# Sixteen gathers of segment ends moved into each edge convolution, and the start of a convolution moved into the stage before it

## The chip, the cores and the metric

The kernel runs on one core of a Trainium2 chip. The metric is the device time of one execution in microseconds (us), given as the median of several runs. The profile is of one execution. Its engines are PE (TensorE; PEld is its weight load), DVE (VectorE), ACT (ScalarE), POOL (GpSimd) and SP (SyncE, which here only issues DMAs). SPq, ACTq and POOLq are the DMA-issuing instructions of an engine.

## What is computed

A graph network on 3125 nodes with 96 features and 53125 directed edges, sorted by their target. Four layers follow each other, each with a residual and a layer norm. The second is the one that the change is about: two edge convolutions with a segment maximum.

```python
def _egnn_conv(x, src, dst, edge_attr, W_msg, W_edge, W_root, b):
    msg = x[src] @ W_msg + edge_attr @ W_edge
    agg = jax.ops.segment_max(msg, dst, num_segments=x.shape[0])
    agg = jnp.where(jnp.isneginf(agg), 0.0, agg)
    return agg + x @ W_root + b
...
x = _layernorm(x + _L0_gnn_ref(x, edge_index), axis=-1)      # two hops of the normalised adjacency
c1 = leaky_relu(_egnn_conv(X, src, dst, edge_attr, W1_msg, W1_edge, W1_root, b1))
c2 = leaky_relu(_egnn_conv(c1, src, dst, edge_attr, W2_msg, W2_edge, W2_root, b2))
x = _layernorm(x + c2)                                       # the second layer
x = _layernorm(x + _L2_gnn_ref(x, edge_index), axis=-1)      # sixteen hops
x = _layernorm(x + _L3_gnn_ref(x, edge_index, ...), axis=-1) # graph convolution, graph norm, another
```

## The kernel before

Nodes lie in 25 tiles of 125 (`P` by `T`); a node array is [125, 25, 96]. The program is a row of stages. Each stage is a block in which all five engines run their own instruction lists, joined by semaphores; between two blocks stands a barrier of all engines, so a block starts when the last engine has finished the one before. In order of time:

1. `build_counts` makes the dense count matrix, degrees and the row in which each node's segment ends.
2. `hops` "l0": two hops, PE-bound. Beside them `AttrHalves` splits the edge attributes into two 16-bit halves: SP loads `l0a_raw` (L642), POOL casts and subtracts (L665, L671), SP stores the halves (L649, L653), 50 rounds through 3 buffers. Behind these on SP stand the ten stores of the state, `state_parked` (L808).
3. `node_product` "c1w" (L934 on): PE turns node tiles (L1011) and multiplies them with W_msg and W_root (L1044); ACT copies the turned tiles (L1053) and writes the high halves of the messages (L1086); DVE writes their low halves (L1129) and the root term (L1131). SP stores `messages` in five cuts (L998), ACT stores `root_parked` (L1078). At the end SP and ACT wait until these stores have landed.
4. `edge_conv` "c1": 26 iterations of 16 tiles of 128 edges. In each, POOL fetches the messages' rows of 11 tiles by indirect DMA (L1240) into `gathered`, which holds two iterations; the other 5 tiles are taken by PE with one-hot matrices (L1273), which DVE makes (L1339) from the source numbers that SP loads (L1190) and ACT offsets (L1392). PE adds attributes and rows in `c_msg` (L1252 to L1262), DVE takes the running maximum along the edges (L1349), PE turns it back (L1300), ACT copies it (L1407) and stores it to `running_max` in DRAM (L1409), 104 groups of 512 edges. `room` (L1225) lets POOL run at most two iterations ahead of PE. At the end ACT waits for its last stores.
5. `node_product` "c2w": now each group of five node tiles must first be put together. POOL gathers the row at which each node's segment ends from `running_max`, one indirect DMA a tile, 25 in all (L1449); SP loads the root term (L1455); DVE adds them and applies leaky ReLU (L1461, L1462). Then turns and products as in c1w. The groups are put into DVE's list between the products by `groups_before` (L971), so that a turn of four tiles waits for the group that holds the last of them.
6. `edge_conv` "c2", as 4.
7. `sixteen_and_one` "l2": first the same 25 gathers with root and state loads, then per group DVE's sum, norm and scaling; PE starts when two groups have gone through. Then sixteen hops and the first product of the last layer, PE-bound throughout.
8. `node_product` "g2w" and `hops` "g2".

The heads of an edge convolution in code (SP, then ACT); DVE's part is three small operations on the edge weights (L1357 to L1361) and then the first one-hots:

```python
for k in range(4):
    sp.dma_start(wf[32 * k:32 * k + 32, :], c["w"][w_edge]).then_inc(s_w, 16)
load_srcs(0, TE)
load_srcs(1, TE)
...
act.wait_ge(s_init, 1)
offset_srcs(0)
act.wait_ge(s_we, 2)
act.wait_ge(s_hot, NC)
offset_srcs(1)
...
evacuate(0)
```

## Time and profile before

| | |
|---|---|
| median of 3 runs | 2112.2 us (2110.45 to 2113.62) |
| the profiled execution's own time | 2111.14 us |
| its span on the core | 2109.1 us |
| busy share of the span | PE 91%, PEld 89%, DVE 61%, ACT 32%, POOL 35% |
| instructions | 55767, of these POOL 756, PE 22813 |
| mean granted clock of TensorE | 0.958 of full speed |

Stages in the trace, us from the span's start: hops "l0" to 234.6; c1w 236.1 to 254.3; the first edge convolution from 259.1, its products from 266.2; c2w from 650.1 to 694.6; the second edge convolution from 698.7, its products from 705.6; the last layers from 1088.5. The stage after the second convolution has its first product at 1117.8 and PE has little idle time from there to 2101.

How to read it: a busy share is an average over stages. PE is the bound in the hops, which are half of the span; what the change touches lies around and inside the two edge convolutions, where PE, POOL and the gaps between the blocks matter one by one. In the rows below, a row of the timeline is: start, length, engine, line, operation, out<-in, shapes, count, and in brackets how long the engine had been idle before it and what ended that. Several neighbours of one kind are merged into one row (x10), whose length then runs from the first start to the last end.

### The profile page before, as it was taken

What the parts mean: (1) busy time and instruction counts of PE and PEld (TensorE: products, weight loads), DVE (VectorE), ACT (ScalarE), POOL (GpSimd) and SP (SyncE); (2) the same over time, 40 slices, a digit from 0 to 9 for tenths busy, and PEclk for the clock granted to TensorE, in tenths of its full rate; (3) what the DMA queues carried; (4) which work ended last, traced back from release to release, by engine and by line L of the source; (5) the groups of instructions that cost most, each with busy time, mean ns of one, the idle gap of its engine ahead of it and who ended that gap; (6) DMA issues with size and microseconds to landing.
All of it is one profiled execution on the core that took longest, in us unless ns stands there. A gap on an engine that the chain in (4) does not pass through costs nothing. (4 is left out here: it accounts for less than half of the span.)

```text
span 2109.1 us, 55767 instructions
## 1 busy us (share of the span) xinstructions
PE 1910.3 (91%) x22813; PEld 1868.7 (89%) x22813; DVE 1277.6 (61%) x3480; ACT 670.2 (32%) x1913; POOL 734.3 (35%) x756
## 2 busy tenths in 40 slices
PE   4579699999994799999956999999999999999968
PEld 3579689999994699999956999999999999999958
DVE  8955578888883588888857444444444444446435
ACT  6843322222221122222212333333333333334234
POOL 2467277777764577777742000000000000000000
PEclk9899899999996899999987999999999999999979
DMA  3034456666664466666650000000000000000001
GB/s 82 1 89 136 114 136 173 168 169 175 166 167 107 118 169 168 177 168 166 177 138 22 2 2 2 2 2 2 2 2 2 2 2 2 2 2 2 2 3 24
DMA packets 150815, 160.32 MB, mean 76 GB/s; under 512 B 43421, under 2 KB 139288, under 8 KB 150561
## 3 DMA queue, kind: packets, MB, share of 16 engines
q1 hardware_dynamic: 98169, 80.74, 14.6%
q0 software_dynamic: 20464, 32.18, 8.1%
q10 hardware_dynamic: 31928, 43.84, 5.8%
q8 instruction: 180, 2.95, 0.6%
q14 instruction: 74, 0.61, 0.1%
HBM read 100.90 MB, written 55.75 MB: 74 GB/s over the span
## 5 line engine op out<-in xcount | busy, mean ns | idle before, releaser
L1240 POOL DMA_INDIRECT c_gathered<-messages,idx_all x572 | 560.2, 979 | 174.9 <-issue 138.3
L1273 PE MATMUL c_taken<-rows,c_hot 125*128 125x192 f16 x6500 | 572.7, 247 | 25.2 <-DVE c_hot L1339 25.2
L1273 PEld LDWEIGHTS c_taken<-rows,c_hot 125*128 125x128 f16 x6500 | 537.0, 98 | 26.1 <-issue 25.8
L1503 PE MATMUL l_ps<-rows,counts 125*128 125x192 f16 x5625 | 471.4, 248 | 40.1 <-DVE rows L1579 39.6
L1503 PEld LDWEIGHTS l_ps<-rows,counts 125*128 125x128 f16 x5625 | 468.2, 99 | 42.1 <-DVE rows L1579 40.8
L1339 DVE TENSOR_SCALAR c_hot<-c_offset_srcs 125x640 f16<-125x640 f16 x1300 | 381.2, 349 | 97.3 <-PE c_taken L1273 84.8
L1503 PE MATMUL l_ps<-l_u,counts 125*128 125x192 f16 x5000 | 413.8, 246 | 0.0
L1503 PEld LDWEIGHTS l_ps<-l_u,counts 125*128 125x128 f16 x5000 | 412.6, 98 | 0.0
L1606 DVE SCALAR_TENSOR_TENSOR l_uf<-l_ps,l_cf,l_wide 125x96 f32<-125x96 f32 x400 | 127.1, 318 | 325.7 <-ACT l_wide L1546 325.6
L1349 DVE TENSOR_TENSOR_SCAN c_scanned<-c_mask,c_scanned,c_msg 96x512 f32<-96x512 bf16 x208 | 264.9, 1273 | 34.9 <-PE c_msg L1262 26.2
L1546 ACT ACTIVATE l_wide<-l_ps,l_cl 125x96 f32<-125x96 f32 x400 | 135.9, 340 | 299.7 <-PE l_ps L1503 299.0
L1407 ACT ACTIVATE c_back<-c_tr 128x384 f32<-128x384 f32 x208 | 102.0, 490 | 402.1 <-PE c_tr L1300 386.9
L1612 DVE TENSOR_TENSOR l_uf<-l_uf,l_wide 125x96 f32<-125x96 f32 x400 | 103.0, 258 | 13.6
L1300 PE MATMUL c_tr<-ident,c_scanned 96*128 96x96 f32 x832 | 103.3, 246 | 4.7 <-DVE c_scanned L1349 4.7
L1550 ACT ACTIVATE l_u<-l_uf 125x96 f16<-125x96 f32 x200 | 56.6, 283 | 135.4 <-DVE l_uf L1612 135.4
L1399 ACT ACTIVATE c_evacuated<-c_taken 128x384 f16<-128x384 f32 x156 | 62.5, 435 | 114.1 <-PE c_taken L1273 102.2
L1615 DVE SCALAR_TENSOR_TENSOR l_u<-l_u,l_uf 125x96 f16<-125x96 f16 x200 | 51.8, 259 | 69.8 <-ACT l_u L1550 69.8
L1550 ACT ACTIVATE rows<-l_uf 125x96 f16<-125x96 f32 x175 | 49.5, 283 | 118.4 <-DVE l_uf L1612 118.4
L1300 PEld LDWEIGHTS c_tr<-ident,c_scanned 96*128 96x128 f32 x832 | 81.1, 141 | 5.7 <-ACT c_back L1407 5.7
L453 PE MATMUL count_ps<-b_hot,b_low 125*128 125x125 f16 x625 | 53.1, 238 | 34.3 <-DVE b_hot L562 33.9
L1252 PE MATMUL c_msg<-c_attr,c_we 128*96 128x512 f16 x208 | 79.5, 382 | 4.9 <-DMA c_attr<-attr_halves 4.8
L405 ACT CAST counts<-count_ps 125x500 f16<-125x500 f32 (+1 forms) x157 | 77.9, 638 | 15.5 <-PE count_ps L441 15.4
(268 smaller groups left out, 1789.5 us busy)
## 6 DMA issues: line engine op xcount, KB each, us to landing
running_max<-c_back ACTq DMA_DIRECT2D x208, 192.0 KB
c_attr<-attr_halves SPq DMA_DIRECT2D x412, 64.0 KB
c_mask<-segment_mask SPq DMA_DIRECT2D x206, 96.0 KB
c_gathered<-messages,idx_all POOLq DMA_INDIRECT x572
c_srcs<-sources SPq DMA_DIRECT2D x50, 160.0 KB
l0a_raw<-in_ea_t SPq DMA_DIRECT2D x50, 132.8 KB
attr_halves<-l0a_hi SPq DMA_DIRECT2D x50, 66.4 KB, 2.0
attr_halves<-l0a_lo SPq DMA_DIRECT2D x50, 66.4 KB, 2.1
```

The costliest lines, as they stand in the source:

```text
L1240: pool.indirect_dma_start(out=gat[:, i % 2, j, :], out_offset=None, in_=c["y_d"], in_offset=bass.IndirectOffsetOnAxis(ap=idx_all[:, i * IT ...
L1252: pe.matmul(msg[0:F, k, :], we[:, :], attr[:, n % AHEAD, :], start=True, stop=False)
L1273: return pe.matmul(acc[:, (NB * i + j // 2) % ACCS, j % 2 * (2 * F):(j % 2 + 1) * (2 * F)], hot[:, slot + k, j * ET:(j + 1) * ET], y[:, t, :],
L1300: last = pe.transpose(tr[0:ET, g % 2, j * F:(j + 1) * F], scanned[0:F, g % 2, j * ET:(j + 1) * ET], ident[0:F, 0:F])
L1339: last = v.tensor_scalar(hot[:, SLOTS[h % len(SLOTS)] + k, :], off[:, :], float(t * P - SRC_MID), None, ALU.is_equal)
L1349: v.tensor_tensor_scan(scanned[0:F, k, :], mk[:, n % AHEAD, :], msg[0:F, k, :], scanned[0:F, 1 - k, GW - 1:GW], ALU.add, ALU.max).then_inc ...
L1407: act.activation(back[:, g % 2, :], tr[0:ET, g % 2, 0:GT * F], ACT.Copy, scale=1.0 / YS).then_inc(s_back, 1)
L1503: return pe.matmul(ps[:, t % HB, 0:2 * F], at[:, k, t * P:t * P + 128], u[hop % 2][:, k, :], start=(k == 0), stop=(k == T - 1), skip_group ...
L1546: act.activation(clo[:, b, :], ps[0:P, b, F:2 * F], ACT.Copy, scale=(cl if hop < count else cl_next)[:, t:t + 1]).then_inc(s_clo, 1)
L1550: act.activation(u[(hop + 1) % 2][:, t, 0:F], uf[:, t, :], ACT.Copy, scale=1.0 / LO).then_inc(s_hi, 1)
L1606: v.scalar_tensor_tensor(uf[:, t, :], ps[0:P, b, 0:F], (cf if hop < count else cf_next)[:, t:t + 1], clo[:, b, :], ALU.mult, ALU.add).then ...
L1612: v.tensor_tensor(uf[:, t, :], uf[:, t, :], xa[:, t, :], ALU.add).then_inc(s_uf, 1)
```

## The change

- The array of rows, `conv_rows` [128, 25, 192] of 16-bit values, is now kept for the whole program. It holds the state in the first layer, in a convolution the gathered rows (22 of its 25 tiles) and part of the evacuated ones, and after it the segment ends as [128, 25, 96] of 32 bits. So result tile t lies where gathered tile t lay.
- When POOL has issued all 286 gathers of messages, it goes on inside the same block with 16 of the 25 gathers of segment ends (`EARLY`), in five pieces of 4, 4, 3, 4 and 1. Ahead of each piece it loads a number from `need` and waits for the message group that last read these rows and for as many stores to `running_max`, on both parities, as the number says. The number is made by three DVE operations in the first convolution, one value per node tile, and loaded by SP in iteration 2. The 9 other gathers stay where they were.
- `ConvHead`: the load and scaling of the edge weights, the first load of sources and its offset are now done in `node_product`. On SP the five loads stand ahead of the stores of messages; on ACT the offset stands first in its list; on DVE the three weight operations stand ahead of everything; POOL does the iota.
- `node_product` no longer waits for its stores. In the convolution POOL waits for the 10 stores of messages ahead of its first gather, DVE for the 10 stores of the root term after three of its eight chunks of one-hots, ACT ahead of its first evacuation.
- In the hops "l0" SP also writes 16 blocks of zeros (196608 bytes each) over the last 16 groups of `running_max`, one ahead of each of the first 16 rounds of the halves; POOL clears the source.

The core of the diff:

```diff
+EARLY = 16
+CUTS = (0, 6, 12, 18, 22, T)
+N_STORED = 32 * (len(CUTS) - 1)
+CLEARED = 16
...
         with ExitStack() as s1:
-            xs = s1.enter_context(nc.sbuf_tensor("x_state", [P, T, F], F32))
-            build_counts(ctx, src, dst, xs, x)
-
+            head = ConvHead(ctx, s1)
+            head.begin("c1h", "W1_edge")
+            node_product(ctx, "c1w", xs, "W1_msg", "W1_root", "b1", y16=y, parked=stored, head=head)
+            result = ConvResult(ctx, "c1r", rows)
+            edge_conv(ctx, "c1", y, result, head, ends=True)
+            head.begin("c2h", "W2_edge")
             with ExitStack() as st:
-                hs = hop_state(ctx, st, "l0", teleports=False)
-                stored = hops(ctx, "l0", hs, xs, 1.0, 0.0, 2, norm=xs, out=xs_d, halves=AttrHalves(ctx, st, "l0a"), later=True)
-            node_product(ctx, "c1w", xs, "W1_msg", "W1_root", "b1", y16=y, parked=stored)
-        edge_conv(ctx, "c1", "W1_edge", y, ends=True)
-        with ExitStack() as st:
-            c1 = st.enter_context(nc.sbuf_tensor("c1", [128, T, F], F32))
-            conv = ConvResult(ctx, st, "c1r", c1)
-            node_product(ctx, "c2w", c1[0:P, :, :], "W2_msg", "W2_root", "b2", y16=y, conv=conv)
-        edge_conv(ctx, "c2", "W2_edge", y)
+                node_product(ctx, "c2w", result.res[0:P, :, :], "W2_msg", "W2_root", "b2", y16=y, conv=result, head=head)
+            result = ConvResult(ctx, "c2r", rows)
+            edge_conv(ctx, "c2", y, result, head)
...
             load(n)
         for n in range(NPREP):
             at_n = slice(n * PREP, (n + 1) * PREP)
+            if n < CLEARED:
+                sp.wait_ge(self.s_zeros, 1)
+                sp.dma_start(self.scan_v[EP // GW - 1 - n, :, :], self.zeros[:, :]).then_inc(self.s_cleared, 16)
             sp.wait_ge(self.s_hi, n + 1)
             sp.dma_start(self.to_d[0][:, at_n], self.hi[:, n % DEEP, :]).then_inc(self.s_put_hi[n % DEEP], 16)
...
                     for a, b in zip(cuts, cuts[1:]):
                         sp.wait_ge(s_o, -(-b // per))
                         for ps in (slice(0, WHOLE), slice(WHOLE, P)):
-                            sp.dma_start(yv[ps, a:b, :], y[ps, a:b, :]).then_inc(s_st, 16)
-                    sp.wait_ge(s_st, 32 * (len(cuts) - 1))
+                            sp.dma_start(yv[ps, a:b, :], y[ps, a:b, :]).then_inc(head.s_y, 16)
                     if parked:
                         sp.wait_ge(*parked)
 
...
                         act.wait_ge(s_o, -(-z // per))
                         for ps in (slice(0, WHOLE), slice(WHOLE, P)):
-                            act.dma_start(c["root_d"][ps, a:z, :], root[ps, a:z, :]).then_inc(s_parked, 16)
+                            act.dma_start(c["root_d"][ps, a:z, :], root[ps, a:z, :]).then_inc(head.s_root, 16)
 
                     done, left = 0, list(zip(cuts, cuts[1:]))
                     for b, r in enumerate(batches):
+                    head.vector(v, wf)
                 if graph_norm:
                     for i, r in enumerate(turns):
...
+        self.w_edge = w_edge
+        self.s_w, self.s_wf, self.s_we, self.s_init, self.s_srcs, self.s_off, self.s_y, self.s_root = (
+            self.c["sem"](f"{tag}_{n}") for n in ("w", "wf", "we", "init", "srcs", "off", "y", "root"))
+
+    def load_srcs(self, sp, i, width):
+        sp.wait_ge(self.s_off, i + 1)
+        at_edge = (i * IT + FROM_POOL) * ET
+        sp.dma_start(self.srcs[:, 0:width], self.c["src_d"][:, at_edge:at_edge + width]
+                     .to_broadcast([128, width])).then_inc(self.s_srcs, 16)
+
+    def offset_srcs(self, act, i):
+
+        act.wait_ge(self.s_srcs, 16 * i + 16)
+        act.activation(self.off[:, :], self.srcs[0:P, :], ACT.Identity, bias=self.lane[:, 0:1]).then_inc(self.s_off, 1)
+
+    def sync(self, sp, wf):
+        for k in range(4):
+            sp.dma_start(wf[32 * k:32 * k + 32, :], self.c["w"][self.w_edge]).then_inc(self.s_w, 16)
+        self.load_srcs(sp, 0, self.TE)
+
+    def gpsimd(self, pool):
+        pool.sem_inc(self.s_off, 1)
+        pool.iota(self.lane[:, :], pattern=[[0, 1]], base=0, channel_multiplier=-1,
+                  allow_small_or_imprecise_dtypes=True).then_inc(self.s_init, 1)
+
+    def scalar(self, act):
+        act.wait_ge(self.s_init, 1)
+        self.offset_srcs(act, 0)
+
+    def vector(self, v, wf):
+        we = self.we
+        v.wait_ge(self.s_w, 64)
+        v.tensor_scalar(wf[:, :], wf[:, :], YS, None, ALU.mult).then_inc(self.s_wf, 1)
+        v.wait_ge(self.s_wf, 1)
+        v.tensor_copy(we[:, :], wf[:, :]).then_inc(self.s_we, 1)
+        v.wait_ge(self.s_we, 1)
+        v.tensor_tensor(we[64:AE, :], wf[64:AE, :], we[64:AE, :], ALU.subtract).then_inc(self.s_we, 1)
+
+
...
+        def taken_rows(j, n):
+
+            k = (j // 2 * 2) % 4
+            return tak[:, j - 2:j - 2 + n, :] if k else rows[:, 2 * FROM_POOL + j - j // 4 * 2:2 * FROM_POOL + j - j // 4 * 2 + n, :]
+
...
                 for s in (s_msg, s_scan, s_tr, s_back):
                     pool.sem_inc(s, GT)
...
+                pool.wait_ge(s_need, 16)
+                if ends:
+                    pool.wait_ge(s_none, 17)
+                pool.sem_inc(s_gate, 1)
+                for k in range(2):
+                    for g, tiles in enumerate(by_dma):
+                        early = [k * FROM_POOL + j for j in tiles if k * FROM_POOL + j < EARLY]
+                        if early:
+                            stored = pool.value_load(need[0:1, early[-1]:early[-1] + 1], min_val=32, max_val=16 * (N_IT * GT // 2 + 1))
+                            pool.wait_ge(s_msg, (N_IT - 2 + k) * GT + g + 1 + GT)
+                            pool.sem_inc(s_gate, 1)
+                            for parity in range(2):
+                                pool.wait_ge(s_st[parity], stored)
+                                pool.sem_inc(s_gate, 1)
+                            for t in early:
+                                result.gather(pool, t)
 
...
+                one_hots(0, 0, 1, 2)
+                v.wait_ge(head.s_root, N_STORED)
+                one_hots(0, *range(3, NC))
                 v.memset(scanned[0:F, 1, GW - 1:GW], 0.0).then_inc(s_zero, 1)
                 v.wait_ge(s_zero, 1)
-                v.wait_ge(s_w, 64)
-                v.tensor_scalar(wf[:, :], wf[:, :], YS, None, ALU.mult).then_inc(s_wf, 1)
-                v.wait_ge(s_wf, 1)
...
-                offset_srcs(0)
-                act.wait_ge(s_we, 2)
                 act.wait_ge(s_hot, NC)
-                offset_srcs(1)
+                head.offset_srcs(act, 1)
+                act.wait_ge(head.s_root, N_STORED)
                 if ends:
...
 
 
-    def __init__(self, c, st, tag, res, root=None):
-        self.c, self.res = c, res
-        self.root = st.enter_context(c["nc"].sbuf_tensor(f"{tag}_root", [P, T, F], F32)) if root is None else root
+    def __init__(self, c, tag, rows):
+        self.c, self.rows, self.res, self.root = c, rows, rows[:, :, :].bitcast(F32), None
         self.s_maxima = [c["sem"](f"{tag}_maxima{g}") for g in range(T // G)]
         self.s_root = [c["sem"](f"{tag}_root{g}") for g in range(T // G)]
         self.s_ready = c["sem"](f"{tag}_ready")
 
+    def gather(self, pool, t):
+        pool.indirect_dma_start(out=self.res[:, t, :], out_offset=None, in_=self.c["scan_d"],
+                                in_offset=bass.IndirectOffsetOnAxis(ap=self.c["end_idx"][:, t:t + 1], axis=0),
+                                ).then_inc(self.s_maxima[t // G], 16)
+
     def gpsimd(self, pool):
-        for t in range(T):
-            pool.indirect_dma_start(out=self.res[:, t, :], out_offset=None, in_=self.c["scan_d"],
-                                    in_offset=bass.IndirectOffsetOnAxis(ap=self.c["end_idx"][:, t:t + 1], axis=0),
-                                    ).then_inc(self.s_maxima[t // G], 16)
+        for t in range(EARLY, T):
+            self.gather(pool, t)
 
```

Two places show how the lists move. POOL, first edge convolution to the next stage (`c_gathered` before and `conv_rows<-messages` after are the gathers of messages; `<-running_max` those of segment ends). Before:

```order
L1215 UNCONDITIONAL_BRANCH
L1222 IOTA c_lane 125x1
L1240 DMA c_gathered<-messages,idx_all 128x192 x286
L1184 UNCONDITIONAL_BRANCH
L100 ISA
L1093 UNCONDITIONAL_BRANCH
L1449 DMA c<-running_max,end_idx 128x96 x25
```

and in the changed kernel:

```order
L1316 DMA conv_rows<-messages,idx_all 128x192 x286
L1329 TENSOR_LOAD c_need
L1329 ISA x2
L1533 DMA conv_rows<-running_max,end_idx 128x96 x4
L1329 TENSOR_LOAD c_need
L1329 ISA x2
L1533 DMA conv_rows<-running_max,end_idx 128x96 x4
L1329 TENSOR_LOAD c_need
L1329 ISA x2
L1533 DMA conv_rows<-running_max,end_idx 128x96 x3
```

Of the 25 gathers behind the block's end (a branch), 16 stand ahead of it now, each piece behind a load of a number. ACT at the start of c1w, before:

```order
L1048 UNCONDITIONAL_BRANCH
L1053 ACTIVATE c1w_xt<-c1w_pt 96x500 x2
L1086 ACTIVATE rows<-c1w_py 125x2x96 x2
L1053 ACTIVATE c1w_xt<-c1w_pt 96x500
L1086 ACTIVATE rows<-c1w_py 125x2x96 x2
```

and in the changed kernel:

```order
L1069 UNCONDITIONAL_BRANCH
L1190 ACTIVATE head_offset_srcs<-head_srcs,head_lane 125x640
L1074 ACTIVATE c1w_xt<-c1w_pt 96x500 x2
L1109 ACTIVATE rows<-c1w_py 125x2x96 x2
L1074 ACTIVATE c1w_xt<-c1w_pt 96x500
```

The offset, which waits for the load of sources, stands ahead of the copies without which PE has nothing to multiply. c2w is built in the same way.

## Rows read from the trace of the kernel before

**Rows 1.** Timeline of hops l0 and c1w; columns as told above, in time and profile
```profile
225.57 9.82 SPq L808 DMA_DIRECT2D state_parked<-x_state  x10
...
233.32 1.29 DVE L757 TENSOR_SCALAR x_state<-x_state,l_n_less,l_n_y 125x96 f32<-125x96 f32 x5
...
236.89 0.32 SPq L992 DMA_DIRECT2D c1w_b_row<-in_w_b  x1
...
240.20 2.92 PE L1044 MATMUL c1w_py<-c1w_w,c1w_xt 96*125 96x192 f32 x8 [2.24 <-DMA c1w_b_row<-in_w_b]
```

**Rows 2.** Timeline, end of c1w and head of the first edge convolution
```profile
254.30 1.73 ACTq L1078 DMA_DIRECT2D root_parked<-c1w_root  x3
...
260.42 1.06 POOL L1240 DMA_INDIRECT c_gathered<-messages,idx_all  x1 [0.58 <-issue]
...
260.91 4.64 SPq L1190 DMA_DIRECT2D c_srcs<-sources  x2
...
264.35 0.83 ACT L1392 ACTIVATE c_offset_srcs<-c_srcs,c_lane 125x640 f16<-125x640 f16 x1 [10.94 <-DMA c_srcs<-sources]
...
266.15 11.80 PE L1273 MATMUL c_taken<-rows,c_hot 125*128 125x192 f16 x125 [13.09 <-DVE c_hot L1339]
```

**Rows 3.** Waits of SP's own queue: engine line, released by, us in total, times, longest
```profile
SPq L978 <- DMA messages<-rows: 5.5, 2, 2.8
```

**Rows 4.** Timeline of POOL in the first edge convolution; its last message gather is 627.40
```profile
386.83 0.95 POOL L1240 DMA_INDIRECT c_gathered<-messages,idx_all  x1 [0.30 <-PE c_taken L1273]
...
587.12 1.01 POOL L1240 DMA_INDIRECT c_gathered<-messages,idx_all  x1 [0.30 <-PE c_taken L1273]
...
627.40 0.94 POOL L1240 DMA_INDIRECT c_gathered<-messages,idx_all  x1 [0.30 <-issue]
```

**Rows 5.** Timeline, end of the first edge convolution and c2w
```profile
647.12 0.33 ACTq L1409 DMA_DIRECT2D running_max<-c_back  x1
...
650.06 4.07 SPq L1455 DMA_DIRECT2D c1r_root<-root_parked  x10
...
659.09 0.66 DVE L1461 TENSOR_TENSOR c1r_root<-c1r_root,c 125x480 f32<-125x480 f32 x1 [13.26 <-DMA c<-running_max,end_idx]
...
666.97 2.77 PE L1044 MATMUL c2w_py<-c2w_w,c2w_xt 96*125 96x192 f32 x8
...
673.27 2.77 PE L1044 MATMUL c2w_py<-c2w_w,c2w_xt 96*125 96x192 f32 x8
...
694.36 0.25 DVE L1131 TENSOR_TENSOR c1r_root<-c2w_py,c2w_b_row 125x96 f32<-125x96 f32 x1
```

**Rows 6.** Timeline of SP and DVE where SP reads two loop counts and starts a loop
```profile
77.61 0.13 DVE L552 TENSOR_SCALAR b_further<-b_rounds 1x1 int32<-1x1 f32 x1
...
80.70 0.33 SPq L303 DMA_DIRECT2D b_win<-edge_values  x1
```

**Rows 7.** Windows: stretch us, busy us and count by engine, PE clock, DMA share, GB/s
```profile
121.00:165.00 44.00, 41.39 (x471) 41.01 (x472) 25.82 (x48) 13.52 (x41) 32.88 (x41) 0.91 0.47 129
...
668.00:684.00 16.00, 10.61 (x38) 9.46 (x37) 6.37 (x16) 3.73 (x9) 10.52 (x12) 0.50 0.31 73
```

**Rows 8.** DMA queue, kind: packets, MB, share of 16 engines; q10 carries ACT's stores
```profile
q10 hardware_dynamic: 31928, 43.84, 5.8%
```

**Rows 9.** Timeline of the second edge convolution: first and last message gather, first product
```profile
699.97 0.95 POOL L1240 DMA_INDIRECT c_gathered<-messages,idx_all  x1 [0.53 <-issue]
...
705.55 6.64 PE L1273 MATMUL c_taken<-rows,c_hot 125*128 125x192 f16 x57 [12.13 <-DVE c_hot L1339]
...
1065.08 0.94 POOL L1240 DMA_INDIRECT c_gathered<-messages,idx_all  x1 [0.30 <-issue]
```

**Rows 10.** Timeline, start of sixteen_and_one
```profile
1088.49 0.75 SPq L1455 DMA_DIRECT2D l_wide<-root_parked  x2
...
1096.74 0.66 DVE L1461 TENSOR_TENSOR l_wide<-l_wide,l_u 125x480 f32<-125x480 f32 x1 [7.50 <-DMA l_u<-running_max,end_idx]
...
1103.07 0.66 DVE L1461 TENSOR_TENSOR l_wide<-l_wide,l_u 125x480 f32<-125x480 f32 x1 [2.58 <-DMA l_u<-running_max,end_idx]
```

120 lines of the change are left out of this document (68 added, 52 removed).

## The prediction

> **What bounds the kernel now.** The busy shares say PE everywhere, but they are averages; the change touches neither the hops nor the 26 iterations of a convolution as such, so I went to the timeline at the seams, then to POOL's row of gathers, then to SP's waits. Three things are to be seen. First, a seam costs about 12 us without products: the last root store of c1w is issued at 256.03 (254.30 + 1.73), the first product of the convolution starts at 266.15 [rows 2]. The block waits for stores to land (SP up to 2.8 [rows 3]), then for weights, sources (3.44 from issue at 260.91 to the offset at 264.35), offset 0.83 and one-hots. Second, behind a convolution DVE waits 13.26 for the first five segment ends in c2w [rows 5], and 7.50 and 2.58 in the next stage [rows 10]. Third, POOL is not idle enough to be ignored: a gather is 0.94 and the 0.30 behind it, so an iteration of 11 takes it at least 13.7; the first nine took 14.05 each (260.42 to 386.83), the next fourteen exactly 14.31 (to 587.12) [rows 2, 4]. That steady 14.31 I read as PE's pace, to which the limit of two iterations holds POOL. Its last gather starts at 627.40, 23 before the block ends.
>
> **The sum, step by step**, against the profiled execution's 2111.14.
>
> *Zeros in the hops.* SP's halves are through at 225.57, when the ten state stores begin; the last two need the norm that ends at 234.61 [rows 1]. Eight stores at some 0.4 (ten loads take 4.07 [rows 5]) must be out by then, which leaves 5.8 of slack. A block of zeros is a store of the form of ACT's: those took 5.8% of 16 engines times 2109.1 over 31928 packets [rows 8], 61 ns a packet, so 128 packets over 16 engines are 0.5 and the sixteen 7.8. Nothing hidden: +2.0; all of it in free time of the DMA engines, which are busy 0.47 there [rows 7]: 0. I take the middle, **+1.0**. POOL's clearing is one instruction in 11 us in which POOL has 0.25 of the time free [rows 7].
>
> *c1w.* ACT's list now begins with an offset that needs sources loaded behind seven small DMAs. SP is through with the third at 237.21 [rows 1]; four more at 0.41 give 238.9, then 3.4 and 0.83 as in rows 2: 243.1. Only then comes the first copy of turned tiles, some 0.6 (an estimate: 500 columns where the offset has 640), so products start at 243.8 for 240.20 [rows 1]. **+3.7**, between 3.0 (copy overlapped) and 4.5. POOL's iota and DVE's weights lie inside that wait.
>
> *First convolution.* Between two blocks the barrier costs 0.7: state stores end at 235.39, SP's third load of the next block is at 236.89, less two issues [rows 1]. So the block starts at 256.7 and PE, one-hots being 1.0 ahead of it (265.18 to 266.15 [rows 2]), at 257.9: 8.2 earlier. But POOL must see the stores landed, 256.03 + 2.8 [rows 2, 3], and gathers from 259.3, only 1.1 earlier. The gathers are needed at PE's new time; eleven of them, 3.4 to land by the sources' row, are there at 275.2, and the third message group, some 19 behind PE's start, asks at 277: I see no stall, with 2 to spare. From here POOL decides: 9.5 behind the pace at which PE held it, it gets its own, between 13.7 and the 14.05 seen while unheld. I take 14.0, near the measured end: last gather at 259.3 + 25 x 14.0 + 12.5 = 621.8, 5.6 earlier. Behind it come 16 gathers at 1.25 (20.0), the 0.94 of the last, 0.7 barrier and five loads of a number. No row shows such a load on POOL; SP needed 2.96 for two of them, three loops and a third load [rows 6], so one is between 0 and 1.0, and with no nearer row I take 0.5, 2.5 in all. Block end 621.8 + 24.1 = 645.9 for 650.06: **-4.2**. PE's side would end at 647.12 - 8.2 plus the 2.9 that follow now [rows 5], 641.9, so POOL's tail is the new end of the block. Its waits for messages and stores cost nothing: tile 15 ends about 64% through the edges, stored long before. DVE's and ACT's waits for the root stores end at 258.8, when DVE has just made its three chunks. The Trainium skill (DMA: Bandwidth & Descriptors, "Latency and other measured facts") gives a floor of about 600 ns for such a load; by that the five are 3.0 and each block ends 0.5 later.
>
> *c2w.* Here 16 of 25 segment ends are there at the start, but others aren't. SP issues ten root loads (4.07), three weights, four edge weights (2.9) and the sources, at 7.0; offset done at 11.2. DVE now waits for the edge weights ahead of its first group, to about 9.6, adds two groups (4 x 0.66), 12.3, and PE turns: products 13.4 into the block for 16.9 (650.06 to 666.97 [rows 5]). After that the pace is 6.30 per group (666.97 to 673.27), and I credit nothing against it: five gathers are 6.25, but turn 1.1, two products' batches 2.8, ACT 0.3, DVE 0.6 and the next group 1.4 are 6.2 in a ring as well (small ones estimated from c1w's and these rows), because `groups_before` puts the group behind the batch. Rows 7 show why it is slow: PE 66% busy at a granted 0.50, the 1.2 GHz level. **-3.8**. The Trainium skill (TensorE: Matmul & The Clock Gate, "What's actually happening") says that the throttled state is the default and activity releases it; without gather waits it would speak for the 2.4 GHz level here. The row with PE at 66% shows no release, and the ring keeps that share.
>
> *Second convolution.* The same: PE 7.8 earlier, POOL 1.1 (699.97 to 698.9), last gather 698.9 + 350 + 12.5 = 1061.4 for 1065.08 [rows 9], block end 1085.5 for 1088.49 [rows 10]: **-3.0**.
>
> *Start of the sixteen hops.* DVE's first group waits for root rows only, some 3.1 after their issue at 1088.49, for 1096.74; the 2.58 ahead of the second go too [rows 10]. Afterwards DVE is never kept by a gather. **-7.7**, between 6.5 and 8.5. The nine gathers left are out 11 us into the block, ahead of the fourth group.
>
> Nine gathers left in c2w cost nothing for the same reason; the doubled use of `conv_rows` adds no instruction.
>
> Sum: +1.0 + 3.7 - 4.2 - 3.8 - 3.0 - 7.7 = **-14.0**, 2097. The profiled execution lies 1.1 under the median of the runs, 2112.2; I leave that in the range. A measurement of this kernel can tell 0.2%, 4.2 us, from no change: faster is below 2108.0, slower above 2116.4.
>
> **The rivals.**
> *POOL doesn't catch up (slower).* If 14.31 is POOL's own pace beside a busy DVE and not PE's hold, the earlier PE gives nothing back and the tail stands behind it in full. With loads at 1.0 the blocks end at 259.3 + 357.8 + 12.5 + 26.6 = 656.2 and at 1095.8: +6.1 and +7.3, sum +6.6, **2118**. Each 0.1 of pace is 5.0 us over both convolutions, so the sign turns at 14.28. For it: fourteen iterations at 14.31. Against: their evenness, their releaser PE, and 14.05 earlier. Chance 0.10; another 0.10 for paces of 14.15 to 14.28, **2107**.
> *The clock rises in c2w.* A ring with turn 0.6 and products 1.5 at 2.4 GHz is 4.4; some four rings save 7: sum -21, **2090**. Against: rows 7. Chance 0.15. With POOL at 13.7 and free loads, both blocks ending with PE, it would be 2081, the far end.
> *The zeros are in the way.* If every load of attributes had to wait for a whole block of zeros, at the 3.4 of the sources' load [rows 2], sixteen cost 54 less 5.8: sum +33, **2144**. The order on SP speaks against it: each round's load is issued ahead of the next zeros. The Trainium skill (DMA: Bandwidth & Descriptors, "Issuing engines are not separate DMA queues") has all issuers share 16 DMA engines, so zeros are never free where those are full; here they are half free. Chance 0.03.
>
> **How the numbers follow.** My forecast, paces up to 14.15, has 0.62. Faster: 0.62 + 0.15 and half of the 2107 case, 0.82. Slower: the part of the first rival beyond 2116.4 and the zeros, 0.07. The same: 0.11. The range runs from the clock case with a faster POOL, 2084, to the 2107 case and its upper side, 2110; it leaves out the slower cases and the far end.
>
> **What would show it.** POOL's last gather of messages near 621.8 + 4.7 (the two stages ahead are later), then pieces of segment ends with gaps of 0.5 to 1 and the next block within 1 us of the last; The first product of each convolution 2 us after the last store issued in the stage before, where it was 10. c1w's first product at about 244.8, with ACT idle on a DMA. c2w still at 0.50 for most of its length and some 27 us from first product to last root term. The first group of the sixteen hops some 3 after the block's start, with no gather wait on DVE. I am wrong if POOL's iterations stay at 14.31 from the start, if the halves' end moves past 231, or if c2w's clock is 1.0.

## The result: 0.24% slower, where 0.7% faster was forecast

| | before | changed |
|---|---|---|
| median of 20 runs each | 2110.89 us (2106.37 to 2116.13) | 2115.42 us (2111.32 to 2120.7) |
| ratio | | 1.0024, 95% interval 1.0018 to 1.0031 |
| the profiled execution's own time | 2111.14 us | 2115.44 us |
| its span | 2109.1 us | 2113.6 us |
| mean granted clock of TensorE | 0.958 | 0.956 |
| POOL instructions | 756 | 757 |

The forecast was 2097, with a range of 2084 to 2110. The result lies above it. The change made the kernel slower: the interval leaves out 1, though its lower end is just inside the 0.2% that I had called the same.

Where the time went, stage by stage, in the two profiled executions. A stage ends where the last instruction of its slowest engine ends or the next block starts, and the spans are differences of such times in the two timelines ([rows 2, 5, 9, 10] and the rows below):

| stretch | before, us | changed, us | difference | forecast |
|---|---|---|---|---|
| start to the end of c1w's root terms on DVE | 254.3 | 257.95 | +3.7 | +4.7 |
| from there to the start of c2w's block | 395.8 | 402.7 | +6.9 | -4.2 |
| c2w, to its last root term | 44.6 | 41.1 | -3.4 | -3.8 |
| from there to the start of sixteen_and_one | 393.9 | 399.3 | +5.4 | -3.0 |
| its head, to PE's first product | 29.3 | 21.6 | -7.7 | -7.7 |
| the rest | 991.3 | 991.0 | -0.3 | 0 |

So four of six rows are right to 1 us, and both convolutions are wrong by 8 to 11 us. First the heads. The timeline of the changed kernel at the start of c1w and across the seam into the first convolution (start, length, engine, line, operation, what it waited for):

```profile
235.55 1.87 PE L1032 MATMUL c1w_pt<-ident,conv_rows 125*96 125x125 f32 x8 [7.11 <-PEq L809]
241.77 0.83 ACT L1190 ACTIVATE head_offset_srcs<-head_srcs,head_lane 125x640 f16<-125x640 f16 x1 [10.08 <-DMA head_srcs<-sources]
243.22 2.89 PE L1065 MATMUL c1w_py<-c1w_w,c1w_xt 96*125 96x192 f32 x8 [5.80 <-ACT c1w_xt L1074]
...
258.01 1.56 ACTq L1101 DMA_DIRECT2D root_parked<-c1w_root  x3
260.15 0.34 SPq L1184 DMA_DIRECT2D head_srcs<-sources  x1
...
261.16 5.12 PE L1366 MATMUL c_taken<-rows,c_hot 125*128 125x192 f16 x31 [4.41 <-DVE c_hot L1432]
262.48 1.16 POOL L1316 DMA_INDIRECT conv_rows<-messages,idx_all  x1 [26.75 <-DMA messages<-rows]
```

The product at 243.22 waits for ACT, which waits for the sources: 3.0 later than in [rows 1], the lower end of what was forecast (3.7, from 3.0 to 4.5). In return the first one-hot product starts 1.6 behind the last root store (259.57), where it was 10.1 in [rows 2]. POOL's first gather is 2.1 later than before, since it waits for the stores of a stage that ended 3.7 later.

Now the end of the convolution. POOL's timeline:

```profile
629.75 0.94 POOL L1316 DMA_INDIRECT conv_rows<-messages,idx_all  x1 [0.30 <-PE c_taken L1366]
631.00 0.94 POOL L1533 DMA_INDIRECT conv_rows<-running_max,end_idx  x1 [0.30 <-issue]
...
649.72 0.94 POOL L1533 DMA_INDIRECT conv_rows<-running_max,end_idx  x1 [0.30 <-issue]
660.64 1.60 SPq L1543 DMA_DIRECT2D c2w_root<-root_parked  x4
660.74 0.13 POOL L1199 IOTA head_lane<- 125x1 f32 x1 [10.07 <-POOLq L105]
```

The early gathers follow the messages' without a gap and at 1.25 each, so the five loads and their waits cost nothing. But between POOL's last gather (650.66) and the next block (660.64) nothing at all runs for 10 us, on any engine. I had put 0.7 there. A row of the timeline does not say what an engine does while it closes a block; the view of one source line does, and the line is that of the block itself. It lists the queue's own instructions: engine, operation, count, duration in ns (least, median, most), start of the first and of the last. The changed kernel at the end of the first convolution:

```profile
L1267 POOLq DRAIN  x1: 21565/21565/21565, 638.2 to 638.2; - x1
...
L1267 PEldq DRAIN  x1: 550/550/550, 640.7 to 640.7; - x1
...
L1267 ACTq DRAIN  x1: 8/8/8, 644.2 to 644.2; - x1
```

And the same view of the kernel before, at the same place:

```profile
L1184 POOLq DRAIN  x1: 13617/13617/13617, 622.6 to 622.6; - x1
...
L1184 ACTq DRAIN  x1: 8/8/8, 649.2 to 649.2; - x1
```

```profile
DMA packets 0, 0.00 MB, mean 0 GB/s; under 512 B 0, under 2 KB 0, under 8 KB 0
```

The other seam is alike: there the DRAIN starts at 1079.9 and takes 20.3, to 1100.2, 9.1 behind a last gather that ends at 1091.10; the next block starts at 1101.07. Its head went as forecast:

```profile
1103.85 0.66 DVE L1549 TENSOR_TENSOR l_wide<-l_wide,conv_rows 125x480 f32<-125x480 f32 x1 [2.03 <-DMA l_wide<-root_parked]
...
1108.42 0.65 DVE L1549 TENSOR_TENSOR l_wide<-l_wide,conv_rows 125x480 f32<-125x480 f32 x1
```

In c2w the products start 14.2 into the block, and PE's granted clock is 0.50 there, the 1.2 GHz level; it rises to 0.61 on average in the last 16 us (timeline and windows). Over all of PE's work in c2w it is 0.57, in the changed kernel (672.4 to 700.75) as in the kernel before (661.0 to 693.4):

```profile
674.86 2.77 PE L1065 MATMUL c2w_py<-c2w_w,c2w_xt 96*125 96x192 f32 x8
...
680.88 2.77 PE L1065 MATMUL c2w_py<-c2w_w,c2w_xt 96*125 96x192 f32 x8
```

```profile
668.00:684.00 16.00, 8.33 (x28) 6.85 (x28) 6.40 (x15) 3.88 (x8) 3.53 (x4) 0.50 0.11 29
684.00:700.00 16.00, 11.38 (x45) 10.85 (x46) 7.18 (x20) 4.25 (x12) 0.00 (x0) 0.61 0.35 92
```

### The profile page after: what moved, and what is told of

Same layout as the page of the kernel before. It is cut to its first block and busy times, and to the rows that moved or that the text cites. A ratio compares the mean times of both kernels' runs of the same rounds, so it can differ in the third digit from the quotient of the medians.

```text
span 2113.6 us, 55849 instructions
## 1 busy us (share of the span) xinstructions
PE 1909.1 (90%) x22813; PEld 1867.1 (88%) x22813; DVE 1274.3 (60%) x3483; ACT 670.9 (32%) x1913; POOL 732.5 (35%) x757
## 5 line engine op out<-in xcount | busy, mean ns | idle before, releaser
L1316 POOL DMA_INDIRECT conv_rows<-messages,idx_all x572 | 560.1, 979 | 233.5 <-issue 146.9
L1432 DVE TENSOR_SCALAR c_hot<-head_offset_srcs 125x640 f16<-125x640 f16 x1300 | 374.8, 345 | 96.4 <-PE c_taken L1366 89.0
L1591 PE MATMUL l_ps<-conv_rows,counts 125*128 125x192 f16 x5000 | 413.8, 246 | 0.0
L1591 PEld LDWEIGHTS l_ps<-conv_rows,counts 125*128 125x128 f16 x5000 | 412.6, 98 | 0.0
L1355 PE MATMUL c_msg<-ident,conv_rows 128*96 128x128 f16 x728 | 108.9, 219 | 0.0
L1354 PE MATMUL c_msg<-ident,conv_rows 128*96 128x128 f16 x728 | 108.8, 218 | 0.0
L1355 PEld LDWEIGHTS c_msg<-ident,conv_rows 128*96 128x96 f16 x728 | 83.8, 122 | 19.5
L1638 ACT ACTIVATE conv_rows<-l_uf 125x96 f16<-125x96 f32 x200 | 56.5, 283 | 135.8 <-DVE l_uf L1700 135.8
L1703 DVE SCALAR_TENSOR_TENSOR conv_rows<-conv_rows,l_uf 125x96 f16<-125x96 f16 x200 | 51.8, 259 | 69.9 <-ACT conv_rows L1638 69.9
L1354 PEld LDWEIGHTS c_msg<-ident,conv_rows 128*96 128x96 f16 x728 | 86.1, 123 | 0.4 <-DMA conv_rows<-messages,idx_all 0.4
```

The costliest lines, as they stand in the source:

```text
L1316: pool.indirect_dma_start(out=gat[:, i % 2, j, :], out_offset=None, in_=c["y_d"], in_offset=bass.IndirectOffsetOnAxis(ap=idx_all[:, i * IT ...
L1354: pe.matmul(to, row[:, 0:F], ident16[:, :], start=False, stop=False)
L1355: last = pe.matmul(to, row[:, F:2 * F], ident16[:, :], start=False, stop=(j == GT - 1))
L1432: last = v.tensor_scalar(hot[:, SLOTS[h % len(SLOTS)] + k, :], off[:, :], float(t * P - SRC_MID), None, ALU.is_equal)
L1591: return pe.matmul(ps[:, t % HB, 0:2 * F], at[:, k, t * P:t * P + 128], u[hop % 2][:, k, :], start=(k == 0), stop=(k == T - 1), skip_group ...
L1638: act.activation(u[(hop + 1) % 2][:, t, 0:F], uf[:, t, :], ACT.Copy, scale=1.0 / LO).then_inc(s_hi, 1)
```

## The experiments

What had to be found out: whether the hole belongs to gathers in arrears, to a toll of the DRAIN itself, or to the loads and register waits; what the early gathers and the moved head are each worth; and whose pace POOL's 14.2 us for 11 gathers is. Each run stands beside runs of the kernel before on the same chip. The first four ran on a chip on which before takes 2348.16 (15 runs), with 18 us for an iteration of a convolution and PE often waiting for its instructions. Their totals are read against that number only; the DRAINs are read as they stand.

### No early gathers, and five

```diff
-EARLY = 16
+EARLY = 0
```

> EARLY is 0: no segment end is gathered inside a convolution, all else of the change stays (head, zeros, waits for stores). Theory A (gathers in arrears): the block waits for POOL's DRAIN, which lasts until its gathers are really through, some 8 to 9 us behind the last row of the timeline, at 1.33 a gather. Then 16 gathers fewer end the DRAIN of the first convolution at 638.5 for 659.8, ACT's last store (DRAIN of ACT at 644.2) sets the end, and c2w starts at 645.1 for 660.6 (-15.5); the second convolution's block ends 13.3 earlier against its start; the sixteen hops' second group has to wait for ten gathers again (+7.2). Total 2094 to 2096. Theory B (the pace only, as in the prediction, the hole being something else that comes with the head or the new array): the hole stays about 10 us behind POOL's or ACT's last work, c2w starts at 650 or later, total 2105 to 2112.

```diff
-EARLY = 16
+EARLY = 5
```

> EARLY is 5, else as the changed kernel. Theory A: eleven gathers fewer at 1.33 end POOL's DRAIN at 645.1, 0.9 later than ACT's end of 644.2, so c2w starts at 646.0; in the second convolution the DRAIN (1100.2 less 14.6) is 1.3 ahead of ACT's end, so 13.3 are saved against the start; the second group of the sixteen hops waits for five gathers more than now, +2. Total 2115.4 - 14.6 - 13.3 + 2.0 = 2089.5, between 2087 and 2093, faster than both kernels. Theory B (a fixed 10 us follow any gather of segment ends inside the block): POOL's last gather is at 636.9, the hole ends at 647, c2w starts at 647.5, and this is 2091 to 2094 too, so this run prices the version and the lone gather tells A from B.

Measured: 2341.24 with none (ratio to before 0.997, 0.9956 to 0.9984) and 2331.57 with five (0.9922, 0.9901 to 0.9943). Both beat the kernel before, on a chip where the absolute numbers of the expectation don't apply. With none, POOL's DRAIN ended 7.8 behind its last gather and ahead of ACT; with five it ended 8.2 behind, still ahead of ACT. In both the next block started 0.8 behind ACT's DRAIN (with none, 762.09 for 761.3), so the moved head and the new array bring no hole behind ACT. A hole of 10 us behind POOL's last gather would be hidden in both runs, so they don't tell arrears from a toll. What they show is that with none or five of the 16 the change is a gain.

### The loads and waits without the gathers

```diff
                             for parity in range(2):
                                 pool.wait_ge(s_st[parity], stored)
                                 pool.sem_inc(s_gate, 1)
-                            for t in early:
-                                result.gather(pool, t)
...
-        for t in range(EARLY, T):
+        for t in range(T):
             self.gather(pool, t)
```

> The five pieces keep their loads of a number and their waits, but gather nothing; all 25 gathers stand in the next stage. Theory A: loads and waits are the sequencer's and cost nothing, POOL's DRAIN ends at 638 to 639 and the blocks end with ACT, c2w at 645 to 646, total within 1 us of the run with EARLY 0 (2094 to 2096). Theory C (register loads, waits on a register and their extra instructions make the hole): the hole of 10 us stays behind POOL's last wait (644), c2w starts at 654 or later, total 2112 or more.

Measured: 2345.19 (one run, before 2348.16). The end of the first convolution, in POOL's timeline and in the block's line:

```profile
740.98 0.99 POOL L1316 DMA_INDIRECT conv_rows<-messages,idx_all  x1 [1.19 <-remote]
766.56 0.13 POOL L1199 IOTA head_lane<- 125x1 f32 x1 [24.59 <-POOLq L105]
```

```profile
L1267 POOLq DRAIN  x1: 7823/7823/7823, 757.3 to 757.3; - x1
...
L1267 ACTq DRAIN  x1: 8/8/8, 765.6 to 765.6; - x1
```

The block ends with ACT, so theory C falls: loads and waits make no hole. But they hold the DRAIN back until 757.3, and that tells against theory A. By then POOL had been without a gather for 15 us, and the queue of POOL's own DMAs (q0) moved no packet from 744 on. No transfer was in arrears, and the DRAIN took 7.82 all the same: what takes this time begins only when the DRAIN is asked for. The Trainium skill (Perfetto Trace Analysis, "DMA Instruction — SWDGE (GPSIMD)") says that POOL's row of such a DMA ends with its descriptors, not with the data; that would explain a short lag (in the changed kernel the last packet moved at 651.8, 1.2 behind the last row), but not 7.82 us when no data was moving.

### One gather behind PE's last turn

```diff
-EARLY = 16
+EARLY = 1
...
-                            pool.wait_ge(s_msg, (N_IT - 2 + k) * GT + g + 1 + GT)
+                            pool.wait_ge(s_tr, N_IT * GT + GT)
```

> EARLY is 1 and that gather waits until PE has turned its last group (641), so POOL is idle for 11 us ahead of it and then issues one gather. Theory A (arrears of a long row of gathers): the arrears are worked off while POOL is idle, the DRAIN ends 2 to 2.5 behind the lone gather, near 644.5, c2w starts at 645 to 646, total 2094 to 2096. Theory B (a fixed 8 to 10 us behind the last indirect DMA of a block that has had hundreds): the DRAIN ends at 650 to 652, c2w starts 6 to 7 later than in the run with EARLY 0, total 2107 to 2110.

```profile
759.98 0.94 POOL L1533 DMA_INDIRECT conv_rows<-running_max,end_idx  x1 [19.17 <-DMA running_max<-c_back]
769.77 0.13 POOL L1199 IOTA head_lane<- 125x1 f32 x1 [8.85 <-POOLq L105]
```

```profile
L1267 POOLq DRAIN  x1: 9073/9073/9073, 759.8 to 759.8; - x1
...
L1267 ACTq DRAIN  x1: 8/8/8, 761.7 to 761.7; - x1
```

```diff
             head = ConvHead(ctx, s1)
+            phase = ExitStack()
+            ctx["sem"] = phase.enter_context(phase_semaphores(nc))
...
+            ctx["sem"] = sem
             head.begin("c2h", "W2_edge")
...
+            phase.close()
             result = ConvResult(ctx, "c2r", rows)
...
-        sem = st.enter_context(phase_semaphores(nc))
+        sem = c["sem"]
...
-        with nc.Block() as block:
+        with nc.Block(no_gpsimd_drain=True) as block:
```

> All 16 early gathers stay; the convolution's block ends without POOL's DRAIN (semaphores alone join the engines), and the clearing of the semaphores with its own DRAIN is moved behind the c2w block (and left out behind the second convolution). Theory B (the DRAIN's toll, 7.8 us after 286 gathers whether POOL is idle or not and 0.08 more per further gather, is the hole): the hole goes. POOL's sequencer is through with its list at 638.2, long before its last gather, so ACT's 644.2 ends the block, c2w starts at 645 for 660.6 (-15.5); likewise -13.3 at the second convolution, and the sixteen hops keep their early second group. Against a before of 2111: 2115.4 - 28.8 = 2086.6, between 2084 and 2090. Theory A' (the block has to wait for the gathers themselves, the DRAIN only shows it): c2w starts at 651.4, 0.7 behind the last gather, total 2115.4 - 9.2 - 8.4 = 2098. On a chip on which before takes 2348 and POOL is idle in every iteration, both give about 2320.

Measured: 2089.67 (2087.09 to 2090.44; before on this chip 2111.08), ratio 0.9893, 0.9878 to 0.9908. The timeline at the end of the first convolution:

```profile
642.91 0.33 ACTq L1501 DMA_DIRECT2D running_max<-c_back  x1
644.36 0.94 POOL L1537 DMA_INDIRECT conv_rows<-running_max,end_idx  x1 [0.30 <-issue]
645.32 2.83 SPq L1547 DMA_DIRECT2D c2w_root<-root_parked  x7
645.60 0.94 POOL L1537 DMA_INDIRECT conv_rows<-running_max,end_idx  x1 [0.30 <-issue]
```

The hole is gone, and more than the hole: the next block starts at 645.32, 2.4 behind the start of ACT's last store, while POOL is still at the early gathers and goes on past the seam. So the block does not have to wait for the gathers themselves either (theory A' gave 651.4). The block starts 15.3 earlier than in the changed kernel (15.5 expected); the second convolution, from the start of c2w to that of sixteen_and_one, saves 11.9 more (13.3 expected). The edit also moves the clearing of the semaphores and its barrier, but in the changed kernel only 0.8 us lie between the DRAIN's end (659.8) and the next block (660.64), so that is the most that they can hold of the 15.3. DRAIN now stands at the end of c2w, where it starts at 651.4 and is over at 668.6 while PE works to 685.8, so it is hidden.

### The version that beats both kernels

As the one without the DRAIN, and the parts of the head go behind the fourth batch of products:

```diff
                 if w2:
-                    head.scalar(act)
-
                     def park(a, z):
...
                         act.activation(y[:, r.start:r.stop, 0:F], of(r, slice(0, F)), ACT.Copy, scale=YS).then_inc(s_hi, 1)
+                        if b == 3:
+                            head.scalar(act)
...
-                if w2:
-                    v.wait_ge(s_w, n_w)
-                    head.vector(v, wf)
...
                     if w2:
+                        if b == 0:
+                            v.wait_ge(s_w, n_w)
+                        if b == 3:
+                            head.vector(v, wf)
                         v.wait_ge(s_hi, b + 1)
```

> As the kernel without the DRAIN, and in c1w and c2w ACT's offset of the sources and DVE's three operations on the edge weights are put behind the fourth batch of products, where they were first in their lists; DVE waits for the weights behind its first groups. My account of the head: c1w's first product goes from 243.2 back to 240.2 (-3.0); in c2w the first two groups need only root rows and gathers, so they go at 4 into the block and the products, which then wait for the weights, at 8 to 9 into it for 14.2 (-5 to -6). Both stages end earlier by that, total 8 to 9 less than the kernel without the DRAIN. Rival: PE and POOL are bound elsewhere in the convolution (POOL's 14.1 per iteration of gathers), so that an earlier c1w gives nothing at the convolution's end beyond the earlier first gather; then still -3.0, since the message stores are earlier too. Rival 2: the offset in the middle of ACT's list delays a batch by 0.8 and gives 1 to 2 back.

Measured: 2077.52 (2076.02 to 2082.17), ratio to before 0.9844, 0.983 to 0.9857: 34 us under the kernel before and 12 under the last one. Of these 12, 2.1 lie in the hops, where the profiled executions differ (c1w's first turn at 234.63 for 236.76), and 1.1 behind the first product of the sixteen hops; the edit touches neither, so it is worth about 9 (8 to 9 expected). c1w and c2w in this kernel's timeline:

```profile
234.63 1.88 PE L1036 MATMUL c1w_pt<-ident,conv_rows 125*96 125x125 f32 x8 [6.68 <-PEq L813]
238.29 1.96 PE L1069 MATMUL c1w_py<-c1w_w,c1w_xt 96*125 96x192 f32 x5 [1.78 <-DMA c1w_b_row<-in_w_b]
```

```profile
639.86 4.10 SPq L1548 DMA_DIRECT2D c2w_root<-root_parked  x10
...
642.53 0.70 DVE L1554 TENSOR_TENSOR c2w_root<-c2w_root,conv_rows 125x480 f32<-125x480 f32 x1 [6.82 <-DMA c2w_root<-root_parked]
...
648.17 2.28 PE L1069 MATMUL c2w_py<-c2w_w,c2w_xt 96*125 96x192 f32 x6 [1.13 <-DMA c2w_b_row<-in_w_b]
```

c1w's products start 3.7 behind the first turn for 7.7 in the changed kernel, c2w's 8.3 into the block for 14.2. Both now wait for the stage's own weights, not for the next stage's head. The first rival fell: the time saved in c1w reached the convolution's end in full, the block lasting as long as before (384.7 from the first one-hot product to the next block, 384.2 without the move). The second rival fell too: from its first turn or its block's start to its last root term c1w became 3.7 shorter and c2w 6.1, so an offset in the middle of ACT's list gave nothing back.

### Five early gathers again, with the DRAIN

> The kernel with five early gathers again, as a measure of whether the slower chip of the first runs decides. Where before takes 2111: the DRAIN ends 8.24 behind the last gather (the toll by 286 + 5), at 629.75 + 5 x 1.25 + 0.94 + 8.24 = 645.2, 1.0 behind ACT's end, c2w at 646.1, total 2089 to 2091.

Measured: 2090.48 (2089.52 to 2095.39), ratio 0.9908, 0.9893 to 0.9923. DRAIN and ACT at the end of the first convolution:

```profile
L1267 POOLq DRAIN  x1: 21757/21757/21757, 624.8 to 624.8; - x1
...
L1267 ACTq DRAIN  x1: 8/8/8, 645.7 to 645.7; - x1
```

POOL's DRAIN ends at 646.6, 0.9 behind ACT and 1.4 later than expected, since the gathers of messages ended later; the total is in the expected range. One number changed in the kernel as it stood, `EARLY`, turns 0.24% slower into 0.9% faster. In the profiled execution c2w took 38.2 for 41.1 in the changed kernel, at a granted clock of 0.66 (659 to 684) for 0.57, so up to 3 us of its gain may go with the clock and not with the seam.

### No early gathers, with and without the DRAIN

> The kernel without early gathers, on a chip where before takes 2111. It prices the 16 early gathers as the change made them: the DRAIN ends 7.8 behind the last gather of messages (630.7 + 7.8 = 638.5), hidden behind ACT's 644 to 646; c2w starts at 646 to 647.5 for 660.6; the sixteen hops' second group is 7 later into its block. Theory B: 2093 to 2097, so that the early gathers as made cost 19 to 22 us and all the rest of the change gains 15 to 18.

> The kernel without the DRAIN and without early gathers, to price the early gathers by themselves. Theory B: the convolution's block ends with ACT as before, c2w starts where it does in the kernel without early gathers and with the DRAIN (within 1 us: the DRAIN was hidden there), and the sixteen hops' second group waits for its gathers: total 7 to 9 above the 2089.7 of the kernel without the DRAIN and with 16, that is 2097 to 2099. Rival: if leaving the DRAIN out gains something by itself, 2092 or less.

Measured: with the DRAIN 2100.65 (ratio 0.9947, 0.9929 to 0.9965), without it 2101.41 (0.9956, 0.9942 to 0.997). The two don't differ, so leaving the DRAIN out gains nothing where it is hidden. The second came out 2 us above its expectation. The first came out 4 to 8 above, because I had priced the missing early gathers in the sixteen hops alone: they are missed in c2w too, whose second group waits 2.96 for its segment ends, so that c2w takes 2.9 longer; and its profiled execution is 4 longer than the changed kernel's from the first product of sixteen_and_one on, which no part of the edit explains.

```profile
659.88 0.66 DVE L1549 TENSOR_TENSOR c2w_root<-c2w_root,conv_rows 125x480 f32<-125x480 f32 x1 [2.96 <-DMA conv_rows<-running_max,end_idx]
```

The price list of the change, from medians: everything but the early gathers (head, zeros, unwaited stores) 2100.65 for 2109.59, -9; the 16 gathers as the change made them 2115.42 for 2100.65, +15; the same gathers without the DRAIN 2089.67 for 2101.41, -12. (The medians of before differ by up to 1.5 between these rows, so each of the three is good to about 2.)

### One more DRAIN in the middle

```diff
                 pool.sem_inc(s_gate, 1)
+                pool.drain()
                 for k in range(2):
                     for g, tiles in enumerate(by_dma):
```

> The changed kernel with one more DRAIN on POOL, between the last gather of messages and the 16 early ones. If the toll is for what has piled up since the last DRAIN, the new one takes up 7.8 us behind the gather at 629.8 (to 638.5), the 16 gathers follow from there (20.0) and the DRAIN at the block's end has only 16 to settle, 2.0 to 2.6: it ends at 660.5 to 661.1, within 1.5 us of the 659.8 of the changed kernel, total 2115 to 2118. If it is a fixed toll of a block that has had hundreds of gathers, the second one costs 9.1 again: 667.6, total 2130.

Measured: 2123.76 (one run). The added DRAIN, the first early gather and the DRAIN at the block's end:

```profile
L1325 POOLq DRAIN  x1: 19696/19696/19696, 620.5 to 620.5; - x1
```

```profile
641.78 0.94 POOL L1534 DMA_INDIRECT conv_rows<-running_max,end_idx  x1 [9.43 <-DMA running_max<-c_back]
...
660.50 0.94 POOL L1534 DMA_INDIRECT conv_rows<-running_max,end_idx  x1 [0.30 <-issue]
```

```profile
L1267 POOLq DRAIN  x1: 11693/11693/11693, 652.0 to 652.0; - x1
```

The added DRAIN ends at 640.2, 7.8 behind the last gather of messages (which ends at 632.35). The one at the end then ends at 663.6, only 2.2 behind its gather, where it was 9.1. So a DRAIN takes the toll of what came before it off the next one. The total is 6 to 9 above the expectation. In the profiled execution the last gather of messages was 1.7 later than the changed kernel's, and 1.6 more passed behind the new DRAIN before POOL gathered again; the second convolution has such a DRAIN too.

### One gather in eleven left out

The eleventh gather of each iteration from the third on is left out, so that PE takes stale rows there; EARLY is 0.

```diff
+                            if i >= 2 and j == FROM_POOL - 1:
+                                continue
                             pool.indirect_dma_start(
...
-                        pe.wait_ge(s_gat[i % 2][g], 16 * from_dma[g] * (i // 2 + 1))
+                        pe.wait_ge(s_gat[i % 2][g], 16 * (from_dma[g] * (i // 2 + 1) - (i // 2 if g == 2 else 0)))
```

> EARLY is 0, and from the third iteration on the eleventh gather of each iteration is left out (PE takes the stale rows that lie there), so a convolution has 262 gathers. Two questions. Whose is POOL's pace: if POOL's own (10 gathers at 1.28), an iteration of gathers takes 12.8 for 14.1, POOL runs up to its limit of two iterations and then stands idle for about 1 us in each; if PE holds it at 14.1 to 14.3 now, the pace does not change at all from the first iteration on. In either case the end of PE's work moves by less than 1 us if PE is its own bound (640.7), and earlier by several us if the gathers bound it. And the DRAIN: if its toll is 0.082 for each gather over 192, it is 5.8 for 7.8; if it is the same for any long row of gathers, 7.8.

Measured: 2099.55 (one run). POOL's waits in the first convolution (released by, us in total, times, longest) of this kernel, and then of the changed one:

```profile
POOL conv_rows L1318 <- issue: 69.9, 212, 2.4
POOL conv_rows L1318 <- PE c_msg L1357: 22.8, 16, 2.2
POOL conv_rows L1318 <- PE c_taken L1368: 7.6, 25, 0.3
```

```profile
POOL conv_rows L1316 <- issue: 72.6, 238, 0.3
POOL conv_rows L1316 <- PE c_taken L1366: 8.5, 28, 0.3
POOL conv_rows L1316 <- PE c_msg L1355: 3.4, 11, 0.3
```

This is what a POOL looks like that waits for PE: gaps of up to 2.4. In the changed kernel, as in the one before, no gap between two gathers of messages is longer than 0.3, whoever is named as the releaser. In this kernel ten gathers took 12.5 to 12.6 us where POOL was free (the third to the seventh iteration), 1.25 each, and 14.3 in nearly all from the fifteenth on, where it was held. 14.31 is PE's own pace: it is the time from one iteration's first `c_msg` product to the next in most iterations of this kernel, of the changed one and of the one before. The missing gathers didn't shorten PE's work (382.6 us from its first one-hot product to the end of its DRAIN, 380.5 with none missing), so the gathers did not bound PE.

Then why does POOL take more than 13.75 for eleven gathers where it doesn't wait? Because some gathers are longer in themselves. One such gather of the kernel before, and two of the changed one:

```profile
403.65 1.51 POOL L1240 DMA_INDIRECT c_gathered<-messages,idx_all  x1 [0.30 <-PE c_taken L1273]
```

```profile
282.10 1.94 POOL L1316 DMA_INDIRECT conv_rows<-messages,idx_all  x1 [0.30 <-issue]
284.35 2.05 POOL L1316 DMA_INDIRECT conv_rows<-messages,idx_all  x1 [0.31 <-issue]
```

In the kernel before the fourteen even iterations (386.83 to 587.12) have one gather of 1.5 each, the third, and ten of 0.94: POOL is in step with PE there. It isn't the limit of two iterations that keeps it so, for the rows that the gather at 386.83 overwrites had been read by 380.9, 6 us earlier. In the changed kernel the long gathers lie irregularly. What makes them long, and how POOL falls into step, no run shows.

The DRAIN ended 5.1 behind the last gather after 262 gathers, where 5.8 was expected from a straight line.

## Why the prediction was wrong

**The step that failed** is the one that closes both convolutions: "Behind it come 16 gathers of segment ends at 1.25 (20.0), the 0.94 of the last, 0.7 barrier and five loads of a number". The 16 gathers took 19.97. The "0.7 barrier" was 10.0: before it stands POOL's DRAIN, which takes 9.1 after 302 gathers. I had taken the 0.7 from the seam between the hops and c1w, where POOL's last work is arithmetic. Runs that moved the DRAIN (left out: block 15.3 earlier; five gathers: 646.6 for 659.8; one more in the middle: 663.6) all moved the seam with it, until ACT ended the block. The sum is wrong by 9.3 here and by as much at the second convolution (1091.09 to 1101.07 less 0.7). This decides it: with the measured pace of POOL and the 0.7 the sum would be 2104, inside the range.

**The pace of POOL** was mis-sized, by 4.8 us in the first convolution and 2.2 in the second: "it gets its own, between 13.7 and the 14.05 seen while unheld. I take 14.0". It was 14.19, (629.75 - 262.48 - 12.5) / 25, and 14.09 in the second; before it was 14.18 and 14.10, so nothing was caught up. Of the 4.8, 3.5 fell in the first three iterations (45.5 from 262.48 to 307.94, with the two gathers of 1.94 and 2.05); the other 22 took 14.06 each. The reading "That steady 14.31 I read as PE's pace, to which the limit of two iterations holds POOL" had the right number for PE and the wrong cause: the 0.30 beside every gather says that POOL didn't wait, and the limit was 6 us away. The first rival was right that an earlier PE gives nothing back, and wrong that 14.31 is POOL's own pace. It put 2118 by a pace of 14.31, loads of 1.0 and a barrier of 0.7; that this is near the measured time is luck, two terms too large for one too small.

**The loads**: 0.5 each was too much. They run in POOL's queue, ahead of the gathers, and the timeline has no gap for them (this is the changed kernel's line of the load, over both convolutions):

```profile
L1329 POOLq TENSOR_LOAD <-c_need x10: 284/290/782, 617.5 to 1078.5; - x10
```

Half take 0.29 or less, and the first starts at 617.5, 13 us ahead of the gather that it guards: none is on the path. By the floor of 600 ns that I cited from the Trainium skill (DMA: Bandwidth & Descriptors, "Latency and other measured facts") the five would be 3.0; the trace does not agree, with 0.29 in the middle and nothing to be seen in the block's length.

First convolution, forecast against measured, in order: first gather 264.0 for 262.48 (-1.5), 25 iterations and the last eleven +4.8, loads -2.5, DRAIN and barrier +9.3: +10.1, and the block did start 10.0 behind the 650.6 that the terms gave. Second convolution, from the last root term of c2w on: DRAIN and barrier +9.3, pace +2.2, loads -2.5, first gather -0.6: +8.4, the table's 5.4 for -3.0.

**Right**: no cost of the zeros is to be seen (the state stores begin at 227.32, 1.75 later, in a hop stage that ended 0.5 earlier than before; I had given +1.0, and the ends of this stage in the kernels with zeros on the faster chip differ by 2.6, so a microsecond can't be told), and the third rival's +33 is refuted; c1w's first product 3.0 for 3.7, held by the sources' offset as told; the first one-hot product 1.6 behind the last store for 2; c2w -3.4 for -3.8 with the clock as in the kernel before (0.57 in both over PE's work), which settles the second rival; the head of the sixteen hops -7.7 for -7.7. Two sums were written down a little off: c1w's terms give 243.7 and so +3.5 where +3.7 stands, c2w's 13.4 for 16.9 is -3.5 where -3.8 stands; together 0.1.

The range was too narrow because all its cases shared the 0.7: no rival asked what POOL has to do between its last gather and the barrier, although the change made POOL the last engine in a convolution's block.

## What to carry to other kernels

When a change makes another engine the last one in a block, read how that engine closes a block, on the line of the block in the trace of before: its DRAIN is there, hidden or not. Work that is moved to POOL's idle end is free only until POOL's last gather plus its DRAIN reaches the engine that ends the block; here that was about five gathers (0.9 behind ACT; between five and sixteen nothing was tried), unless the block is joined by semaphores alone. And a releaser's name says that an engine is held only if the wait beside it is longer than the gap that every instruction has; where it is not, look at how long the rows themselves are.
